# Transposed attention scores: four-pass fp32 products replaced by three fp16 products of high and low parts

## The reference

```
h = rms_norm(layer_norm(x)) ;  q, k, v = split(h @ w_qkv.T)      # 16 heads of 64
q, k = rope(q), rope(k)
k = concat(persist_mem, k) ;  v = concat(persist_mem, v)         # 4 extra keys: 260 in all
attn = softmax(where(causal, q @ k.T / 8, -inf))
x = x + (attn @ v) @ w_out.T
```

## Time and profile before

| | before |
|---|---|
| median of 3 executions | 1206.99 us |
| the profiled execution's own time | 1204.28 us |
| its span, first to last instruction | 1202.5 us |
| TensorE busy | 1136.8 us, 95% |
| VectorE busy | 942.5 us, 78% |
| ScalarE busy | 684.7 us, 57% |
| GpSimd busy | 655.0 us, 54% |
| mean granted TensorE clock | 0.977 |

### The profile page before, as it was taken

The page is one execution under the profiler, slowest core; times in us unless marked ns, Lnnn a source line. Parts: engine busy times, 40 slices in busy tenths (PEclk is TensorE's granted clock), DMA queues, the critical chain, the costliest instruction groups (busy, mean ns, idle before and its releaser), DMA issues.

```text
span 1202.5 us, 36709 instructions
## 1 busy us (share of the span) xinstructions
PE 1136.8 (95%) x13099; PEld 802.8 (67%) x13099; DVE 942.5 (78%) x3302; ACT 684.7 (57%) x1474; POOL 655.0 (54%) x1082
## 2 busy tenths in 40 slices
PE   3889999999999999999999999999999999999981
PEld 2556767667776766777677677767667777766661
DVE  5677888888877888787878878877788878788636
ACT  3555565656555566655656665565555565565533
POOL 3544555556555555655555556555556556555425
PEclk8899999999999999999999999999999999999995
DMA  5222333332233333233333323333332333333204
GB/s 200 86 83 79 108 104 112 107 108 83 84 104 98 116 106 109 70 96 106 99 115 109 107 73 92 105 108 108 104 97 78 98 108 95 112 103 97 65 10 140
DMA packets 77990, 119.80 MB, mean 100 GB/s; under 512 B 13041, under 2 KB 35954, under 8 KB 77682
## 3 DMA queue, kind: packets, MB, share of 16 engines
q1 hardware_dynamic: 68722, 111.18, 30.7%
q10 hardware_dynamic: 9088, 6.29, 1.8%
HBM read 41.53 MB, written 8.78 MB: 42 GB/s over the span
## 4 chain that ended last, share of the span: by engine, by line
PE 76%; DVE 6%; DMA 5%; ACT 4%; issue 4%; POOL 3%; SPq 2%; DVEq 0%; ACTq 0%; POOLq 0%
PE bank_pv L1044 13%; PE bank_st L1007 12%; PE bank L953 12%; PE bank_sum L1080 8%; PE bank L971 6%; PE bank_sum L1063 6%; PE bank_sm L985 5%; DMA rope_c<-rope_b 4%; PE bank_st L1010 3%; PE bank L1166 2%; PE bank L1168 2%; ACT xn L600 2%; PE bank_sm L993 2%; POOL qk L385 2%; PE bank L1095 1%
## 5 line engine op out<-in xcount | busy, mean ns | idle before, releaser
L385 POOL TENSOR_TENSOR qk<-rope_a,rope_c 128x512 f32<-128x512 f32 x256 | 336.0, 1312 | 269.7 <-DMA rope_c<-rope_b 264.5
L763 DVE CUSTOM_DVE_ANT_0 masked<-bank_sm,mask_q 128x132 bf16<-128x132 f32 (+1 forms) x1024 | 307.6, 356 | 43.5 <-PE bank_sm L985 42.9
L521 ACT ACTIVATE prob<-bank_st 128x776 f32<-128x776 f32 x256 | 208.5, 814 | 160.0 <-PE bank_st L1010 159.2
L752 DVE TENSOR_TENSOR rope_a<-bank,cos 128x512 f32<-128x512 f32 x256 | 174.1, 680 | 125.1 <-PE bank L953 116.2
L1007 PE MATMUL bank_st<-qk 64*128 64x256 f32 (+1 forms) x2048 | 239.4, 326 | 0.1
L376 POOL TENSOR_SCALAR_AFFINE_SELECT prob<-prob 128x256 f32<-128x256 f32 x256 | 113.9, 445 | 227.5 <-ACT prob L521 226.4
L1044 PE MATMUL bank_pv<-prob,v_sb 128*64 128x256 f32 (+1 forms) x2048 | 224.7, 340 | 2.2 <-POOL prob L378 1.8
L506 ACT ACTIVATE qk_h<-qk 128x512 f16<-128x512 f32 x256 | 160.1, 625 | 98.0 <-POOL qk L385 96.9
L1007 PEld LDWEIGHTS bank_st<-qk 64*128 64x128 f32 x2048 | 154.8, 188 | 31.7 <-issue 0.8
L753 DVE TENSOR_TENSOR rope_b<-bank,sin 128x512 f32<-128x512 f32 x256 | 173.7, 679 | 0.0
L1044 PEld LDWEIGHTS bank_pv<-prob,v_sb 128*64 128x64 f32 x2048 | 124.5, 136 | 72.7 <-issue 31.4
(11 more groups left out here) (190 smaller groups left out, 1712.5 us busy)
## 6 DMA issues: line engine op xcount, KB each, us to landing
rope_c<-rope_b SPq DMA_DIRECT2D x512, 128.0 KB, 2.1
rinv<-linv_scratch SPq DMA_DIRECT2D x124, 256.0 KB, 4.5
out<-x_sb SPq DMA_DIRECT2D x16, 256.0 KB, 2.5
linv_scratch<-linv SPq DMA_DIRECT2D x62, 64.0 KB, 2.0
x_sb<-x ACTq DMA_DIRECT2D x28, 128.0 KB, 4.8
pre<-w_qkv_t ACTq DMA_DIRECT2D x1, 1024.0 KB, 5.5
v_sb<-pm_v SPq DMA_DIRECT2D x64, 8.0 KB
v_end<-v_end_scratch SPq DMA_DIRECT2D x64, 8.0 KB
```

Source lines behind the costliest of these rows:

```text
L385: G.tensor_tensor(qk[:, s, :].rearrange("p (u n) -> p u n", u=2)[:, :, 0:NT], rope_a[:, s % 4, :].rearrange("p (u n) -> p u n", u=2), rope ...
L521: A.activation(prob[:, s % 4, :, :], ps_st[:, :, 0:SCOL], ACT.Exp).then_inc(S["exp_done"], 1)
L752: V.tensor_tensor(rope_a[:, s % 4, :], proj_bank(j, s)[:, :], cos[:, :], ALU.mult)
L763: ins = V.tensor_tensor_reduce(masked[:, e, c0:c0 + n], ps_sm[:, e, c0:c0 + n], mask_q[:, c0:c0 + n], 1.0, LOWEST, ALU.add, ALU.max, top[: ...
```

## The change

Queries and keys are kept as two fp16 tiles, the rounded value `qk_h` and the rest `qk_l`, and the transposed scores are the sum of three fp16 products (high by high, high by low, low by high) instead of one fp32 product; the small products of the last keys likewise. The rest is computed by a subtraction `low`: on GpSimd for pairs 1, 2, 3, 4, 6 and 7, placed behind `causal` two steps after the pair's rope step, in step 1 ahead of `factors`; on VectorE for pairs 0 and 5, in steps 2 and 7, behind `maxima`. The fp32 tile `qk` becomes a ring of four pairs without the extra keys, so `rope_add` waits for `low` of the pair four before, and `hi` now waits for the transposed scores of the same pair one sequence earlier. `end_keys` copies two fp16 tiles and moves from steps 1 and 6 to steps 3 and 7. TensorE waits for `low` before each `scores_t`.

```diff
--- before.py
+++ after.py
@@ -114,11 +114,13 @@
-        qk = sb("qk", [P, NPAIR, 2 * NKEY], f32)
-        k_end = sb("k_end", [P, NPAIR * NEND], f32)
+        qk = sb("qk", [P, 4, 2 * NT], f32)
+        k_end_h = sb("k_end_h", [P, NPAIR * NEND], f16)
+        k_end_l = sb("k_end_l", [P, NPAIR * NEND], f16)
         top_t = sb("top_t", [P, 2, NT], bf16)
         qk_h = sb("qk_h", [P, NPAIR, 2 * NKEY], f16)
+        qk_l = sb("qk_l", [P, NPAIR, 2 * NKEY], f16)
         v_sb = sb("v_sb", [P, 2, DI], f32)
         v_end = sb("v_end", [P, P], f32)
@@ -163,7 +165,7 @@
             "sp_tick pe_tick ld_x0 ld_x1 ld_b0 ld_b1 ld_b2 ld_b3 ld_w ld_wv ld_c ld_ident ld_rope ld_ffn ld_small ld_wo v_pm0 v_pm1 ld_end "
             "casts_act casts_dve casts_pool end_xn end_tr end_hi end_done ve_ready ve_copied ve_stored "
             "h_stats h_rstd h_xn h_tr h_hi_done h_lo_done "
-            "qk_proj qk_read swapped0 swapped1 rope_sum hi_done sm_ready max_done top_tr top_copied "
+            "qk_proj qk_read swapped0 swapped1 rope_sum hi_done lo_done lo_done_dve sm_ready max_done top_tr top_copied "
             "st_ready exp_done causal_done pv_ready raw_done sum_ready linv_done linv_stored spread0 spread1 norm_done y_ready x1_done "
             "v_ready v_done v_end sx_done sx_rstd xn_ready xt_ready xt_hi_done xt_lo_done gate_ready gate_read c_hi_done state_done "
             "end_exp end_summed end_added k_end_done lin_ready pre_done cf_ready cf_done fin_sum fin_sum_pool fin_tanh fin_out fin_out_pool stored "
@@ -198,6 +200,19 @@
             for j in range(NB + 3):
                 body(j, j % 2)
+
+        LOW_DVE = (0, 5)
+        LOW_POOL = tuple(s for s in range(NPAIR) if s not in LOW_DVE)
+
+        def low_sem(j, s):
+
+            if s in LOW_DVE:
+                return S["lo_done_dve"], len(LOW_DVE) * j + LOW_DVE.index(s) + 1
+            return S["lo_done"], len(LOW_POOL) * j + LOW_POOL.index(s) + 1
+
+        def low_parts(s):
+
+            return [t[:, k, :].rearrange("p (u n) -> p u n", u=2)[:, :, 0:NT] for t, k in ((qk_l, s), (qk, s % 4), (qk_h, s))]
         OWN = (slice(0, 64), slice(64, 128))
         def proj_bank(j, s):
@@ -380,12 +395,17 @@
             def rope_add(j, s):
+                if 8 * j + s >= 4:
+                    pool.wait_ge(*low_sem(j - (s < 4), (s - 4) % NPAIR))
+                pool.wait_ge(swapped[s % 2], 32 * (NPAIR // 2 * j + s // 2 + 1))
+                G.tensor_tensor(qk[:, s % 4, :], rope_a[:, s % 4, :], rope_c[:, s % 2, :], ALU.add).then_inc(S["rope_sum"], 1)
+
+            def low(j, s):
+
+                pool.wait_ge(S["hi_done"], NPAIR * j + s + 1)
                 wait(pool, S["st_ready"], NPAIR * (j - 1) + s + 1)
-                pool.wait_ge(swapped[s % 2], 32 * (NPAIR // 2 * j + s // 2 + 1))
-                G.tensor_tensor(qk[:, s, :].rearrange("p (u n) -> p u n", u=2)[:, :, 0:NT],
-                                rope_a[:, s % 4, :].rearrange("p (u n) -> p u n", u=2),
-                                rope_c[:, s % 2, :].rearrange("p (u n) -> p u n", u=2),
-                                ALU.add).then_inc(S["rope_sum"], 1)
+                lo, full, hi_ = low_parts(s)
+                G.tensor_tensor(lo, full, hi_, ALU.subtract).then_inc(S["lo_done"], 1)
             def rstd(cj):
@@ -409,6 +429,10 @@
                         rstd(j - 2)
                     if b:
                         causal(j - 1, s)
+                    if s < 2 and b and NPAIR - 2 + s in LOW_POOL:
+                        low(j - 1, NPAIR - 2 + s)
+                    if s >= 2 and a and s - 2 in LOW_POOL:
+                        low(j, s - 2)
                     if s == 1 and real(j + 1):
                         factors(QT, j + 2, POOL_H * (j + 1))
@@ -478,7 +502,6 @@
             act.wait_ge(S["ld_small"], 64)
             pk = pmk_raw[:, :].rearrange("p (c n) -> p c n", c=NPAIR)
-            cast(A.copy(qk[:, :, NT:NT + NPM], pk))
             cast(A.copy(qk_h[:, :, NT:NT + NPM], pk))
             def mask_cast():
@@ -501,10 +524,10 @@
             def hi(j, s):
                 act.wait_ge(S["rope_sum"], NPAIR * j + s + 1)
-                wait(act, S["sm_ready"], NPAIR * (j - 1) + s + 1)
+                wait(act, S["st_ready"], NPAIR * (j - 1) + s + 1)
                 A.activation(qk_h[:, s, :].rearrange("p (u n) -> p u n", u=2)[:, :, 0:NT],
-                             qk[:, s, :].rearrange("p (u n) -> p u n", u=2)[:, :, 0:NT], ACT.Copy).then_inc(S["hi_done"], 1)
+                             qk[:, s % 4, :].rearrange("p (u n) -> p u n", u=2), ACT.Copy).then_inc(S["hi_done"], 1)
             def exp(bj, s):
                 act.wait_ge(S["st_ready"], NPAIR * bj + s + 1)
@@ -522,10 +545,14 @@
             def end_keys(j, half):
-                act.wait_ge(S["rope_sum"], NPAIR * j + 4 * half + 4)
+                for s in range(4 * half, 4 * half + 4):
+                    act.wait_ge(*low_sem(j, s))
+                act.wait_ge(S["hi_done"], NPAIR * j + 4 * half + 4)
                 wait(act, S["st_ready"], NPAIR * (j - 1) + 4 * half + 1)
-                A.activation(k_end[:, half * KE:half * KE + KE].rearrange("p (s n) -> p s n", n=NEND),
-                             qk[:, 4 * half:4 * half + 4, NKEY + QE:NKEY + NT], ACT.Copy).then_inc(S["k_end_done"], 1)
+                for dst, src in ((k_end_h, qk_h), (k_end_l, qk_l)):
+                    ins = A.activation(dst[:, half * KE:half * KE + KE].rearrange("p (s n) -> p s n", n=NEND),
+                                       src[:, 4 * half:4 * half + 4, NKEY + QE:NKEY + NT], ACT.Copy)
+                ins.then_inc(S["k_end_done"], 1)
             def copy_top(j, half):
@@ -638,9 +665,9 @@
                         hi(j - 1, NPAIR - 1)
                     if s >= 1 and a:
                         hi(j, s - 1)
-                    if s == 1 and b:
+                    if s == 3 and b:
                         end_keys(j - 1, 1)
-                    if s == 6 and a:
+                    if s == 7 and a:
                         end_keys(j, 0)
                     if s == 0 and c:
                         raw_copy(j - 2, p, NPAIR - 1)
@@ -734,7 +761,7 @@
             def scan_starts():
-                dve.wait_ge(S["casts_act"], 14)
+                dve.wait_ge(S["casts_act"], 13)
                 fr = f_raw.rearrange("p (g n) -> p g n", g=8)
                 for u, scale in ((0, WS), (4, WS / 2)):
                     V.scalar_tensor_tensor(f_lo[:, u:u + 4, :], fr[:, u:u + 4, :], scale, f_hi[:, u:u + 4, :], ALU.mult,
@@ -771,6 +798,13 @@
                 wait(dve, S["sum_ready"], 4 * bj)
                 V.tensor_reduce(prob_end_sum[0:64, :, :], prob_end[0:64, bj % 2, :, :, :].rearrange("p e s q -> p e q s"), AX.X,
                                 ALU.add).then_inc(S["end_summed"], 1)
+
+            def low(j, s):
+
+                dve.wait_ge(S["hi_done"], NPAIR * j + s + 1)
+                wait(dve, S["st_ready"], NPAIR * (j - 1) + s + 1)
+                lo, full, hi_ = low_parts(s)
+                V.scalar_tensor_tensor(lo, full, 1.0, hi_, ALU.mult, ALU.subtract).then_inc(S["lo_done_dve"], 1)
             def end_add(cj, par):
@@ -860,7 +894,11 @@
                         maxima(j - 1, s + 5)
                     if s >= 3 and a:
                         maxima(j, s - 3)
+                    if s >= 2 and a and s - 2 in LOW_DVE:
+                        low(j, s - 2)
                     if j == 0 and s == 5:
+                        V.tensor_tensor(qk_l[:, :, NT:NT + NPM], pmk_raw[:, :].rearrange("p (c n) -> p c n", c=NPAIR),
+                                        qk_h[:, :, NT:NT + NPM], ALU.subtract).then_inc(S["casts_dve"], 1)
                         end_low()
                     if s == 0 and n:
                         first_stats(j + 1)
@@ -959,7 +997,7 @@
                 if m == 0 and real(bj + 1):
                     pe.wait_ge(S["h_lo_done"], bj + 2)
                 if bj == 0 and m == 0:
-                    pe.wait_ge(S["casts_dve"], 4)
+                    pe.wait_ge(S["casts_dve"], 5)
                 if bj == 0 and m == 2:
                     pe.wait_ge(S["ve_copied"], 2)
                 if m == 2:
@@ -997,15 +1035,18 @@
                 if isinstance(bj, int) and bj == 0 and s == 0:
                     pe.wait_ge(S["ld_small"], 64)
                     pe.wait_ge(S["ld_wo"], 16)
-                    pe.wait_ge(S["casts_act"], 12)
+                    pe.wait_ge(S["casts_act"], 11)
                 if s % 4 == 0:
                     pe.wait_ge(S["top_copied"], 2 * bj + 1 + s // 4)
                 wait(pe, S["exp_done"], NPAIR * bj + s)
+                QK = (qk_h, qk_l)
+                pe.wait_ge(*low_sem(bj, s))
                 for kc, q0, c0 in CHUNKS:
-                    for e in range(2):
-                        T.matmul(ps_st[:, e, c0:c0 + NT - q0], qk[OWN[e], s, NT + kc * P:NT + (kc + 1) * P],
-                                 qk[OWN[e], s, q0:NT], start=True, stop=False)
```

(14 more changed lines are left out.)

## The result

| | before | after |
|---|---|---|
| median of 4 executions | 1208.28 us | 1240.42 us (1239.09 to 1241.18) |
| the profiled execution's own time, span | 1204.28, 1202.5 us | 1240.11, 1238.0 us |
| TensorE busy | 1136.8 us, 95% | 1102.7 us, 89% |
| GpSimd busy | 655.0 us, 54% | 910.5 us, 74% |

The changed kernel is slower: ratio 1.0267, 95% interval 1.0238 to 1.0297. TensorE is busy 34 us less, and the profiled execution is 36 us longer.

A forecast was written before the change was run, and what follows sets the result against it. TensorE was taken to set the pace, with two slackless chains through GpSimd ending at it. Gain -39, chains +37 and +26 us sum to +24, giving 1231 us against the median 1206.99; range 1190 to 1256.

The forecast's parts named there:

- two waits: TensorE waiting in step 3 for `copy_top`, 1.22 us, and in step 0 for xn, 0.86 us, each some 30 times.
- TensorE's gain: fp16 products in `scores_t` save 0.16 us per pair, 41 us; small last-key products cost 2; net 39 us.
- Rival D: In `scores_t`, weight loads make 132-column products take 0.11 us each, 0.33 instead of 0.17 for three: 1262 us; chance 0.03.
- Price of `low`: One `low` on GpSimd takes 1.27 us, like the undisturbed rope sum; bounds 0.7 or 0.8 to 1.95 us.
- rival B: `low` on GpSimd is cheap, 0.7 us, so both waits shrink: 1195 us, faster than before; chance 0.15.
- Chain 1: Steps 1 to 3: pair 7's `low` delays rope sum, `hi`, `copy_top`, then `scores_for_max`: 1.22 us per iteration, +37 us.
- Chain 2: Steps 6 to 0: pair 4's `low` delays `rstd`, `second_norm`, then `transpose_xn`: 0.86 us, 30 times, +26 us.
- `low` of pairs 0 and 5 on VectorE: at nothing: Steps 2 and 7: 0.68 us each, 64 times, 44 us, hidden in VectorE's 19% of idle time.
- `end_keys` in step 7: On ScalarE, 0.21 us more ahead of `second_norm`, put at nothing because `second_norm` waits for `rstd` anyway.
- narrow range of 1219 to 1243: The forecast's own range of total time, for a `low` from 1.1 to 1.5 us; chance 0.48.
- Rival A: Order within a step has slack that was misread, so TensorE's gain comes whole: 1168 us; chance 0.12.
- rival C: VectorE's four `divide` operations wait for GpSimd, holding output projections in steps 5 and 6: 18 us, 1249 us; chance 0.12.

The follow-up runs named there:

- the split of `spread_linv`: Second half of `spread_linv` issued behind step 3's swap: 1177.55 us without `low`, 1198.63 in the kernel before, 1237.69 in the changed kernel.
- my first four expectations: Changed kernel with `low` of pair 7 moved, pair 4 moved, both moved, or no `low`: expected 1205, 1209, 1174, 1169 us; measured 1221.78, 1218.77, 1200.00, 1203.52.
- the best version: Changed kernel with `low` of pairs 7, 4 and 5 moved, `spread_linv` split, `end_keys` of the first four pairs in step 6: 1176.01 us, ratio 0.9727.

## Why the prediction was right, and where it was not

The forecast was 1231 us, range 1190 to 1256, the mechanism two waits; measured 1240.42 us, with the two waits at their two places.

- **TensorE's gain, 39 us.** Right in its parts: 0.33 and 0.17 us by the starts; the small products of the last keys take about 0.02 us more at each of 64 places, 1 us against the 2 forecast. Rival D is out: 132-column products with new weights follow each other after 0.06 us, so the 107 ns per load of the Trainium skill (TensorE: Matmul & The Clock Gate, LDWEIGHTS) do not bind here.
- **Price of `low`, 1.27 us.** It took 1.16 us undisturbed, within the bounds and far from rival B's 0.7 us. This subtraction into fp16 is thus 0.11 us shorter than the fp32 sum of the nearest row. The estimate of 1.11 us worked out from the Trainium skill (GPSIMD Engine Reference, Elementwise — side-by-side cycle accounting) was nearer to it than that row.
- **Chain 1, 1.22 us.** 1.19 us in the iteration shown; the wait totals 35.1 us against +37 forecast.
- **Chain 2, 0.86 us.** 1.20 us; 39.1 us in total, 36.2 more than before, against +26. **This is the step that failed**, and in it the line "`low` of pairs 0 and 5 on VectorE: at nothing". I asked what VectorE's `low` delays on VectorE and what GpSimd does to VectorE, and not what it does to GpSimd: the last operation of `rstd` lay under it and took 0.47 us more. Moving that one operation gave 13 us of wait back. With 0.47 added, and 0.11 off for the shorter `low`, the sum is 0.86 + 0.47 - 0.11 = 1.22, and 1.20 was measured. `end_keys` in step 7 cost nothing here, as forecast, since `second_norm` idles 0.73 us for `rstd` behind it.
- **Sum.** -39 + 37 + 26 = +24, measured +32 between the medians and +36 between the profiled executions. Chain 2's wait is 10 us more than forecast, chain 1's 3 less. TensorE's busy time fell by 34 and not by 39, but that is no shortfall of the gain: busy time counts drains, and the kernel without `low`, with and without the split of `spread_linv`, has 1102.5 and 1108.4 us for the same products. Part of the nearness is luck. With `low` at its measured 1.16 us my sum would have given 1231 - 30 x 0.22 = 1224 us; the time came back into my narrow range of 1219 to 1243, which was meant for a longer or shorter `low`, through a term that I had put at nothing.
- **Rival A** (slack that I misread) fell with both waits; **rival C** (`divide` waits for GpSimd) is small in the changed kernel, 1.5 us of TensorE's wait for raw, although the mean of a `divide` operation rose from 0.80 to 0.90 us. A wait for `divide` did come, 16.0 us, in the kernel without `low`, so not from the operations that the rival named but by way of the swap.
- **What I had not seen** is the third chain. It did not hurt the forecast, since in the changed kernel it hides behind the wait of step 3. But my statement that without the two waits the gain of TensorE comes whole (1168 us) was wrong by it, and my first four expectations were too low. To a smaller part `end_keys` in step 7 is behind that too: its 0.21 us, hidden while `second_norm` waits for `rstd`, show as soon as that wait is gone.

Open: after the split the kernel before takes 1198.63 us and the best version, in the same job, 1176.01, a gain of 22.6 us, where the starts promise 39 to 40. In the best version TensorE waits 4.1 us more at `transpose_xn` (6.7 against 2.6) and 3.7 more for `divide` (4.2 against 0.5); the remainder was not traced.

## What to carry to other kernels

Before work is added to an engine that is idle for part of the time, follow each chain that ends at the bottleneck and measure its slack step by step: the same operation cost 0.63 us each time in two places of an iteration and nothing in four. Count an operation's effect on the engine that shares its path to SBUF in both directions, and on the smallest operation of a chain above all. When a removed wait gives back less than its length, run the kernel with the whole suspected work left out: what is still missing then belongs to another chain. And an operation that costs nothing behind a wait is not free: `end_keys` showed its 0.21 us as soon as the wait for `rstd` was gone.

## What the hardware showed

- VectorE and GpSimd hold each other up in SBUF for about the rest of the other's operation: `sx_m` of 128x2 took 0.67 us instead of 0.19 beside VectorE's `low`; c_lo took 0.98 us in the median and 0.39 at best; VectorE's `low` (two SBUF inputs) took 1.15 us in the mean and 0.68 alone:

```profile
L807 DVE SCALAR_TENSOR_TENSOR qk_l<-qk,qk_h 128x512 f16<-128x512 f32 x64 | 73.9, 1154 | 0.6 <-ACT qk_h L529 0.6
...
L408 POOL TENSOR_TENSOR qk_l<-qk,qk_h 128x512 f16<-128x512 f32 x192 | 223.3, 1163 | 0.0
```

  The Trainium skill states this (SBUF — State Buffer, Who interferes with whom): GpSimd's ports are VectorE's second pair, under an exclusive lock. The rows agree, and add that the smallest operation waits as long as a large one, which mattered here.
- A swap of two 128 KB DMAs issued behind four of 256 KB released its reader 4.5 us after the end of its issue, the swap ahead of the four 1.6 us after. Two of the four moved behind the swap gave 26 us without `low` and 10 in the kernel before: the place in SyncE's list of a transfer that TensorE does not wait for decided it.
